# First loads in another order, the modulation matrix in three transfers, and products on a constant ahead of the first modulation row

## The reference, cut to what matters

```python
mod = (_silu(L0_c) @ L0_wmod).reshape(1, 6, 1, -1)        # c: 1x256, wmod: 256x1536
sa, ca, ga, sb, cb, gb = (mod[:, m] for m in range(6))
...
h = _layernorm(x) * (1 + ca) + sa                          # x: 1x1024x256
x = x + ga * attention(layernorm(h) * gamma + beta, qkv, o_proj)
h = _layernorm(x) * (1 + cb) + sb
x = x + gb * moe_with_shared_expert(h)
```

## Time and profile before

| | |
|---|---|
| median of 3 runs | 195.94 us (195.86 to 196.1) |
| span of the profiled execution | 195.2 us |
| executions' median over the profiled span | 0.74 us |
| PE busy | 155.4 us (80% of the span) |
| DVE busy | 106.3 us (54%) |
| POOL busy | 72.3 us (37%) |
| ACT busy | 63.8 us (33%) |
| moved by DMA | 33.47 MB, mean 171 GB/s |

### The profile page before, as it was taken

The page is one execution under the profiler, slowest core; times in us unless marked ns, Lnnn a source line. Parts: engine busy times, 40 slices in busy tenths (PEclk is TensorE's granted clock), DMA queues, the critical chain, the costliest instruction groups (busy, mean ns, idle before and its releaser), DMA issues.

```text
span 195.2 us, 2961 instructions
## 1 busy us (share of the span) xinstructions
PE 155.4 (80%) x1002; PEld 109.1 (56%) x1002; DVE 106.3 (54%) x377; ACT 63.8 (33%) x168; POOL 72.3 (37%) x96
## 2 busy tenths in 40 slices
PE   0298679999989999852992149995999969979984
PEld 0164437875558758631840034584877657569763
DVE  1589947459566979982142736792444523300453
ACT  3437876421457165330000125100264435400000
POOL 8129301995000000477776058540003726560000
PEclk9999999999999999999579556999699999999999
DMA  4999999999999900021100000009401101116992
GB/s 123 301 385 393 417 420 378 350 348 349 348 348 348 299 9 0 27 95 50 32 17 11 0 3 11 9 8 291 156 0 33 49 14 54 42 65 250 399 325 104
DMA packets 24670, 33.47 MB, mean 171 GB/s; under 512 B 2817, under 2 KB 19958, under 8 KB 24656
## 3 DMA queue, kind: packets, MB, share of 16 engines
q1 hardware_dynamic: 22352, 30.86, 46.1%
q0 software_dynamic: 2304, 2.44, 3.8%
HBM read 23.45 MB, written 13.83 MB: 191 GB/s over the span
## 4 chain that ended last, share of the span: by engine, by line
PE 30%; DVE 22%; DMA 12%; issue 11%; another core or an unknown queue 10%; ACT 6%; POOL 6%; SPq 1%; POOLq 1%; DVEq 0%; ACTq 0%
PE bank L997 7%; PE bank L1282 6%; DMA w_sb<-results 5%; POOL slots L437 4%; PE bank L1301 3%; DMA w_sb<-in_L_wmod_dram 3%; PE bank L1329 3%; PE bank L1261 3%; DVE bmax L768 2%; DMA arena<-slots 2%; DVE st L679 2%; POOL results L447 2%; DVE rows L789 2%; PE bank L1101 1%
## 5 line engine op out<-in xcount | busy, mean ns | idle before, releaser
L437 POOL DMA_INDIRECT slots<-rows,slot_idx x32 | 31.5, 984 | 52.0 <-DVE slot_idx L868 41.6
L447 POOL DMA_INDIRECT results<-arena,res_idx x16 | 15.6, 975 | 29.3 <-DVE arena L953 24.4
L1127 PE MATMUL bank<-arena 128*128 128x256 f32 x72 | 19.0, 411 | 0.4 <-issue 0.4
L1282 PE MATMUL bank<-w_sb,arena 128*64 128x128 f32 x256 | 17.7, 285 | 0.0
L1282 PEld LDWEIGHTS bank<-w_sb,arena 128*64 128x64 f32 x256 | 14.9, 143 | 2.4 <-issue 1.8
L1127 PEld LDWEIGHTS bank<-arena 128*128 128x128 f32 x72 | 14.3, 206 | 3.0 <-issue 0.9
L997 PE MATMUL bank<-w_sb,h2T 128*128 128x512 f32 x12 | 7.5, 760 | 8.5 <-DMA w_sb<-in_L_wmod_dram 8.5
L966 DVE TENSOR_TENSOR h2T<-h2T,bank 128x256 f32<-128x256 f32 x8 | 3.4, 422 | 15.5 <-ACT h2T L641 15.5
L539 ACT ACTIVATE h2T<-bank,modc 128x128 f32<-128x128 f32 x16 | 6.5, 455 | 14.1 <-PE bank L1135 12.5
L520 ACT ACTIVATE prob<-bank,nmax 128x512 f32<-128x512 f32 (+3 forms) x12 | 6.9, 581 | 12.4 <-DVE nmax L772 12.4
L1245 PE MATMUL bank<-ones_bf,ident_bf 128*128 128x128 bf16 x160 | 9.8, 219 | 1.1 <-issue 1.1
(11 more groups left out here) (155 smaller groups left out, 308.9 us busy)
## 6 DMA issues: line engine op xcount, KB each, us to landing
w_sb<-in_L_ffn_w_dram SPq DMA_DIRECT2D x12, 1024.0 KB, 12.4
results<-prob SPq DMA_DIRECT2D x1, 4096.0 KB, 22.0
w_sb<-results SPq DMA_DIRECT2D x7, 512.0 KB, 7.1
slots<-prob SPq DMA_DIRECT2D x1, 2112.0 KB, 12.1
arena<-slots SPq DMA_DIRECT2D x4, 528.0 KB, 5.5
xin<-in_L_attn_x_dram SPq DMA_DIRECT2D x4, 256.0 KB, 4.6
w_sb<-in_L_wmod_dram SPq DMA_DIRECT2D x1, 1024.0 KB, 9.7
out_dram<-base SPq DMA_DIRECT2D x8, 128.0 KB, 3.5
```

Of the source, the lines that this page charges most:

```text
L437: g.indirect_dma_start(out=slots_d, out_offset=bass.IndirectOffsetOnAxis(ap=slot_idx[:, i, k:k + 1], axis=0), in_=rows[:, i, :], in_offset ...
L447: g.indirect_dma_start(out=results_d, out_offset=bass.IndirectOffsetOnAxis(ap=res_idx[:, r:r + 1], axis=0), in_=ob[:, (r // 2) % 4, (r % 2 ...
L1127: last = t.matmul(bank[6][:, 0:H], probT[:, i % 2, j, :], vo[:, j, :], start=(j == 0), stop=(j == i))
L1282: last = t.matmul(bank[4 + g % 2][CAP * side:CAP * side + CAP, o:o + F], slotT[:, k, CAP * e:CAP * e + CAP], w[:, e, k, :], start=(k == 0) ...
```

## The change

The loads are issued in another order: `x` 0, `wmod_a`, `x` 1, `qkv`, `x` 2, `x` 3, the first half of `wmod_b`, gamma, beta, `o_proj`, the second half of `wmod_b`, gate weights, gate bias. `c` is issued by ScalarE ahead of its table load. `wmod` has three semaphores, and `mod_rows(b)` waits for its own. GpSimd writes `ones_bf` first and the zeros of `prob` after `causal_bf`; SyncE waits for `consts` at 8 for these zeros. TensorE issues 50 products on `ones_bf` before it waits for `silu_c_done` and the first part of `wmod`.

```diff
-        WARM1, WARM2 = 10, 150
+        WARM0, WARM1, WARM2 = 50, 10, 150
...
-            sp.dma_start(cc[:, 0, :], c.rearrange("a (p k) -> p (a k)", k=KT)).then_inc(c_loaded, 16)
             wmod_d = wmod.rearrange("(p k) n -> p k n", k=KT)
-            for j in range(NB):
+            def load_x(j):
                 sp.dma_start(xin[:, 2 * j:2 * j + 2, :], x_d[:, 2 * j:2 * j + 2, :]).then_inc(x_loaded[j], 16)
-                if j == 1:
-                    sp.dma_start(wmod_a, wmod_d[:, :, 0:512]).then_inc(wmod_loaded[0], 16)
+            load_x(0)
+            sp.dma_start(wmod_a, wmod_d[:, :, 0:512]).then_inc(wmod_loaded[0], 16)
+            load_x(1)
             sp.dma_start(qkv_sb, qkv.rearrange("(p k) n -> p k n", k=KT)).then_inc(qkv_loaded, 16)
-            sp.dma_start(wmod_b, wmod_d[:, :, 512:1536]).then_inc(wmod_loaded[1], 16)
+            load_x(2)
+            load_x(3)
+            sp.dma_start(wmod_b[:, :, 0:512], wmod_d[:, :, 512:1024]).then_inc(wmod_loaded[1], 16)
             sp.dma_start(gb_col[:, 0, :], col(gamma)).then_inc(small_loaded, 16)
             sp.dma_start(gb_col[:, 1, :], col(beta)).then_inc(small_loaded, 16)
+            sp.dma_start(wo_sb, o_proj.rearrange("(j p) n -> p j n", p=P)).then_inc(wo_loaded, 16)
+            sp.dma_start(wmod_b[:, :, 512:1024], wmod_d[:, :, 1024:1536]).then_inc(wmod_loaded[2], 16)
             sp.dma_start(gatew_sb[:, :], gate_w).then_inc(small_loaded, 16)
             sp.dma_start(bias_b[:, :], row_bcast(gate_bias)).then_inc(small_loaded, 16)
-            sp.dma_start(wo_sb, o_proj.rearrange("(j p) n -> p j n", p=P)).then_inc(wo_loaded, 16)
-            sp.wait_ge(consts, 1)
+            sp.wait_ge(consts, 8)
...
         def _(pool):
-            g.memset(prob[:, :, :], 0.0).then_inc(consts, 1)
+            g.memset(ones_bf[:, :], 1.0).then_inc(consts, 1)
...
+            g.memset(prob[:, :, :], 0.0).then_inc(consts, 1)
...
         def _(act):
+            a.dma_start(cc[:, 0, :], c.rearrange("a (p k) -> p (a k)", k=KT)).then_inc(c_loaded, 16)
...
             def mod_rows(b):
+                pe.wait_ge(wmod_loaded[b], 16)
...
+            def keep_warm(count):
+                for _ in range(count):
+                    t.matmul(bank[0][:, 0:P], ones_bf[:, :], ones_bf[:, :], start=True, stop=True)
+            pe.wait_ge(consts, 1)
+            keep_warm(WARM0)
             pe.wait_ge(silu_c_done, 1)
-            pe.wait_ge(wmod_loaded[0], 16)
             mod_rows(0)
...
-            pe.wait_ge(wmod_loaded[1], 16)
             mod_rows(1)
```

More of the change, by code:

```diff
@@ L192, in adaln_attention_moe @@
         x_loaded = [sem(f"x_loaded{j}") for j in range(NB)]
-        wmod_loaded = [sem("wmod_loaded0"), sem("wmod_loaded1")]
+        wmod_loaded = [sem(f"wmod_loaded{b}") for b in range(3)]
         qkv_loaded = sem("qkv_loaded")
@@ L379, in _ @@
                             fill=0.0, base=0, channel_multiplier=1).then_inc(consts, 1)
-            g.memset(ones_bf[:, :], 1.0).then_inc(consts, 1)
-            pool.wait_ge(consts, 4)
             g.affine_select(out=ident_bf[:, :], in_=ones_bf[:, :], pattern=[[-1, P]], compare_op=ALU.is_equal,
@@ L387, in _ @@
             g.memset(causal_bf[:, :], 0.0).then_inc(consts, 1)
-            pool.wait_ge(consts, 7)
+            pool.wait_ge(consts, 6)
             g.affine_select(out=causal_bf[:, :], in_=causal_bf[:, :], pattern=[[-1, P]], compare_op=ALU.is_ge,
                             fill=MASKED, base=0, channel_multiplier=1).then_inc(consts, 1)
+            g.memset(prob[:, :, :], 0.0).then_inc(consts, 1)
             lw = lower[:, :, :]
@@ L1095, in scores @@
                     pe.wait_ge(mod_raw, 1)
-                    pe.wait_ge(consts, 8)
+                    pe.wait_ge(consts, 7)
                 n = P * (i + 1)
@@ L1240, in _ @@
                 last.then_inc(shd_mm, 1)
-            def keep_warm(count):
-                for _ in range(count):
-                    t.matmul(bank[0][:, 0:P], ident_bf[:, :], ones_bf[:, :], start=True, stop=True)
             pe.wait_ge(sh_hid, 4)
```

## The result

The changed kernel is slower: 198.81 us median of four executions (196.43 to 199.37) against 195.9 us (194.78 to 196.1), ratio 1.0156 with a 95% interval of 1.0079 to 1.0233. That is +1.5 to +4.6 us around +3.05 us, where +1.07 was forecast; the median lies above the forecast range. The profiled execution has a span of 196.5 us against 195.2 us, so trace against trace shows only 1.3 us of it.

What follows compares the result with a forecast made beforehand. The prediction took the head as bound by VectorE waiting for x 3, not by the first modulation row. Span 195.2 + 1.07 = 196.3, plus 0.74 outside it, gave 197.0 us; 8 in 10 range 195.3 to 198.3.

Steps and rivals of the forecast that it cites:

- +1.07: Later start of VectorE's mod01_evac, 13.35 us and not 12.28, carried whole to the end of the span.
- the forecast range: The forecast time of 196.6 to 197.5 us, chance 0.48; the 8 in 10 range was 195.3 to 198.3.
- Both releases of the second group: VectorE's x_moments(1): x 3 landing and VectorE getting free after x 1's work both come at about 11.25 us.
- The rule of the same set: Loads: x 3 lands once the set that qkv needed before is in, 11.67 less 0.44, so 11.23 us.
- rival C: No change: x 3 lands near 10.2 or later slack takes up the 1 us; 195.9 us, chance 0.08.
- Rival B: TensorE's clock at 1.2 GHz near 14.3 delays wqk and hn_tile, up to 1.2 us more; 198.2 us, chance 0.17.
- Both stops: First loads: x 1 behind wmod_a lands at 7.91 us, x 3 behind qkv at 11.23 us, each holding VectorE.
- no later step waits for a load that the change brings earlier: Chain from mod01_evac to hn_tile and turn_h(0): all moves by the same +1.07 us.
- the 50 products were costed by TensorE's own time at the start alone: TensorE's start: 122 ns each, 6.1 us, over near 7.2 as wmod_a lands, costed at nothing.
- rival D: Head loses 1.07 us, but later low clock stretches and unknown-queue waits shift a microsecond either way; chance 0.10.
- the pause of TensorE: TensorE idle from near 11.0 to 14.3 us, some 3.4 us, in which the clock may fall again.

Runs made afterwards that it cites:

- e7: Kernel before with qkv alone issued between wmod_a and x 2; ratio 1.0075.
- e10: Kernel before with wmod_a alone issued between x 0 and x 1; ratio 1.0114.
- e6: Changed kernel with x 2 and x 3 issued ahead of qkv again; ratio 1.015.
- e9: Changed kernel with its first loads (x 0 to 3, wmod_a, qkv) in the old order, the rest as changed; ratio 1.0001.
- e4: Kernel before with the 50 early products and the GpSimd order of constants they need, old loads; ratio 0.9998.
- e8: Kernel before with wmod_b in two transfers and o_proj between them; ratio 1.0007.
- e13: Kernel before with 100 semaphore waits added on TensorE near the start, no products; ratio 1.0001.
- e2: Changed kernel with c issued first on SyncE again; ratio 1.0111.
- e3: Kernel before with the new order of SyncE's loads alone, c in front; median 200.52 us against 196.88 us, no ratio.
- e5: Changed kernel run again, unaltered, on another chip; ratio 1.0142.
- e11: Changed kernel with 55 more products filling TensorE's pause after the second group of transposes; ratio 1.0032.
- e14: Changed kernel with 52 semaphore waits on TensorE ahead of silu_c_done and 52 in its pause; ratio 1.0156, from three of six executions.
- e15: Changed kernel with its 50 products moved from the start to the pause after the second group of transposes; ratio 1.011.
- e16: Changed kernel run for the third time, unaltered, on another chip; ratio 1.0147.
- e17: Repeat of e11, the changed kernel with 55 more products in TensorE's pause; ratio 1.0015.
- e18: Changed kernel with the old order of its first loads and 100 early products in place of 50; ratio 0.9935.

## Why the prediction was right about the head and wrong in its sum

**The head, step by step, was right.** `x` 1 in at 7.74 (forecast 7.91), `wmod_a` at 6.6 (7.1), `mod_rows(0)` over at 8.7 (9.0), VectorE's second group at 11.17 (11.30), `mod01_evac` at 13.10 (13.35) with no wait for TensorE, `hn_tile` at 22.19 (22.3). Both releases of the second group come together, as worked out. e7 and e10 show each alone, e6 that undoing one of them does not help, e9 that undoing both does. The rule of the same set gave the landing of `x` 3 too: with `c` still in front it is 11.67, and in e7 the group that waits for it starts at 11.52.

**The head's delay reaches the dispatch whole.** From `mod01_evac` to the first dispatch scatter it takes 68.24 us in the kernel before (12.28 to 80.52), 68.34 in the changed one (13.10 to 81.44), and 68.2 to 68.4 in every other trace. So nothing takes it up there, and rival C falls for the head. Rival B's price there is 0.1 us: the clock did fall, `wqk` came at 21.27, but `hn_tile` had only a tenth to wait for it.

**The size of the head's term.** +1.07 is a difference against one trace, `mod01_evac` at 12.28. The loads of the kernel before are in four traces (before, e4, e8, e13): 12.28, 12.00, 10.81, 12.68, mean 11.94. Both stops are in nine (after, e2, e3, e5, e11, e14, e15, e16, e17): eight of them 12.94 to 13.31, e3 14.16, mean 13.26. The term is then 1.3 us, and 1.5 if e3, e13, e14 and e17 are left out. With the old list `mod01_evac` varies by 1.9 us between four traces, so that a difference of 0.2 to 0.4 to the forecast is not a clear one; it was partly luck that one trace gave a term so near. Why the old list varies more than the new one was not looked into. The price of one stop as time is of that size too: +0.75% in e7 and +1.14% in e10 are 1.4 and 2.2 us, with intervals of 0.7 to 0.9 us each way.

**The step that failed** is the one that ends the sum: span 195.2 + 1.07, the head's delay as the only term. All that stands behind the dispatch was put at nothing, in the sentence that no later step waits for a load that the change brings earlier; the 50 products were costed by TensorE's own time at the start alone, and rival D, which had other parts of the kernel move, was given 0.10 and a microsecond either way. The runs showed a ratio of 1.0142 to 1.0156 in three runs of the changed kernel, 2.7 to 3.1 us, of which the head gives 1.3 to 1.5. Some 1.2 to 1.8 us are in no term of the sum. What causes them stays open. The runs show three things about them: they do not come without the order (e9, e4, e8, e13: 0.9998 to 1.0007), nor clearly with the order of the loads alone (e7, e10), and most of the loss goes when the pause of TensorE is filled beside the early products (e11, e17).

**Where the time is in the traces.** e5 and e8 are of one chip, which shows no waits for an unknown queue, and e8 is the kernel before but for the split of `wmod_b`. e5 is 4.4 us longer (189.0 against 184.7): 2.2 in the head (e8's is the earliest of all), nothing from `mod01_evac` to the twenty-first dispatch scatter, -0.2 from there to the last scatter of results, 1.7 in the tail wait, 0.6 from there to the end. TensorE's mean granted clock from 24 us to the last scatter was 0.92 of 2.4 GHz in e5 and 0.94 in e8, and this cost nothing there. So in this pair rival D's middle part fell, and what is left beside the head lies behind the last scatter.

**The tail wait.** Its first half in e5, in the chain of waits:

```profile
166.17 4.02 DMA results<-arena,res_idx
...
170.27 3.44 DMA w_sb<-results
```

and the queues in that first half, e5, 166.17 to 170.27 (packets, MB, share of 16 engines):

```profile
q0 software_dynamic: 96, 0.10, 7.6%
q8 instruction: 1, 0.02, 1.9%
```

e17, with no such packet, in its own first half, 167.11 to 169.36:

```profile
q0 software_dynamic: 99, 0.11, 15.3%
```

Queue 8 brings instructions, 16 KB in a packet, eight packets in the kernel before. That they are TensorE's is read from e13: 100 instructions more on TensorE alone, and the last packet comes at 181.3 where it came at 184.2. In nine traces one of them falls into the tail wait (after, e2, e4, e5, e6, e9, e14, e15, e16), and that wait is 6.08 to 7.56 us, mean 6.75. In the other eleven none does, and it is 5.64 to 5.86, mean 5.74. All nine have the 50 products of 100 instructions (or, in e14, these and the waits); none of the kernels with none, with 100 or with 105 has it. So early products can move a fetch into the place where the kernel waits for a transfer, and this goes with +1.0 us of that wait in 20 traces without an exception. It is not shown by an experiment that moves the fetch alone, since e13 and e14 missed the place.

The Trainium skill (Runtime: NRT & Kernel Launch, Instruction fetch mechanics) says that instructions are fetched in blocks of 16 KiB by the engine's own DMA queue and that crossing a block is mostly hidden. The packets of 16 KB agree. These nine tail waits are longer with one; whether the time is, the runs leave open.

For the longer wait is not yet a longer kernel. e4 and e9 have tail waits of 7.01 and 6.59 and ratios of 0.9998 and 1.0001. From the issue of the last scatter to the end of the span the nine traces take 20.2 to 22.9 us, mean 21.3, and the eleven 19.9 to 21.8, mean 20.8: half of the microsecond is gone by the end, and it is within what either group spreads. The changed kernel's first trace takes 21.0 there and the kernel before 21.4. The chains of waits show why. In the kernel before, the last results are still on their way long after VectorE's first use at 179.60:

```profile
177.85 8.88 DMA w_sb<-results
```

and in e5 TensorE's work follows the first use at once and holds the end:

```profile
173.75 4.41 PE bank L1336 x12
```

In e5 and e6 the 150 products that `keep_warm` puts into this wait were over before it ended: TensorE had nothing to do for 2.55 and 2.37 us and then took up its work at 0.50, 1.2 GHz. In e8 it had nothing to do for 0.84 us, and its clock stayed up. These two are the only traces of the twenty in which the clock is low just behind the first use.

**What stays open.** The head and the half microsecond at the end come to some 2 us of the 2.7 to 3.1, which the intervals allow. But the parts do not add: e4 has the longer tail wait and loses nothing, and e11 and e17 have the late head and lose only 0.3 to 0.6 us, where the head alone would give 1.3 to 1.5. The intervals of these two reach up to 1.4 and 1.0 us. Either something gives them about 1 us, or the order costs less by itself than e7 and e10 say. The traces don't tell: the clock in the pause alone isn't it (e15), nor are more instructions alone (e14, as far as it went).

## What to carry to other kernels

When loads are reordered, write for each consumer the set of loads that must be in before it can go on, in the order in which the consumer asks: a load that moves up pushes back, by its bytes, every one that it passes, and an engine that works in order is held by the first late one of them. Test such an order with all its stops undone together as well as one by one, for two stops that are equally late hide each other (e6). And take a start out of one trace only with the spread that other traces of the same kernel show; here the base was 0.34 us late (12.28 against a mean of 11.94) under a term of 1.07. Last, a delay followed to the dispatch is only the first term: what the change does to the rest of the kernel needs a term or a bound of its own, and a wait that grows counts only if the chain behind it grows with it.

## What the runs showed of the hardware that was not expected

- The landing of the same first loads, from the same list, moved `mod01_evac` between 10.81 and 12.68 us in four traces.
- On two of the five chips the kernel before took 187.25 and 188.12 us, on the other three 195.3 to 196.88. Most of the difference lies between the first and the twenty-first dispatch scatter: 25.8 us (e5 to e8, e17, e18) against 30.8 to 33.6. On the slower chips the chain has waits there, of 1.2 to 14.9 us, that the profile puts to an unknown queue. The longest of e9, in the chain of waits:

```profile
86.81 11.31 another core or an unknown queue
```

  In e5 to e8, e17 and e18 there are none, and GpSimd issues scatter behind scatter. What these waits are was not found.
- 50 products warm TensorE for work that comes soon: `mod_rows(0)` takes 1.95 us in the changed kernel, where it starts 0.15 us after them, 1.95 us in e11, 1.1 us after them, and 3.75 us in e4, 2.8 us after them.
- The same 50 products took 5.51 us in the changed kernel, 5.13 in e11, 4.46 in e9 and 4.35 in e4. How long such products last is not the same in every execution, and with it the gap to the work behind them.
